# A three-layer cross network with gathers on one core: start-up, gathers and tower pieces rearranged, and ScalarE's copies turned round

## The reference

```python
def layer_stack(x0, W0, W1, W2):          # x0: (1024, 32, 16)
    xk, outs = x0, []
    for W in (W0, W1, W2):                # W: (32, 32 or 64, 64)
        xk = relu(einsum('bmd,bhd,mhk->bkd', x0, xk, W))
        outs.append(xk.sum(axis=2))
    return concatenate(outs, axis=1)      # (1024, 192)

e = stack([tbl_f[ids[:, f]] for f in range(32)], axis=1)
h = concatenate([layer_stack(e, W0, W1, W2), dense_ctx], axis=1)
y = relu(relu(h @ W_top1 + b_top1) @ W_top2 + b_top2) @ W_top3
```

## Time and profile before

| | |
|---|---|
| median of 3 runs | 656.71 us (653.54 to 657.66) |
| profiled execution, its own time | 655.87 us |
| its span in the trace | 654.1 us |
| busy: TensorE, VectorE, GpSimd, ScalarE | 574.3, 561.2, 474.0, 230.4 us |

### The profile page before, as it was taken

How to read it: one execution, slowest core, us unless ns; L and a number is a source line. 1 busy time by engine, 2 the same in 40 slices (tenths; PEclk the granted TensorE clock), 3 DMA queues, 4 the chain that set the end, 5 groups by cost and what they waited for, 6 DMA issues and landing times.

```text
span 654.1 us, 7255 instructions
## 1 busy us (share of the span) xinstructions
PE 574.3 (88%) x2752; PEld 202.9 (31%) x2752; DVE 561.2 (86%) x291; ACT 230.4 (35%) x425; POOL 474.0 (72%) x356
## 2 busy tenths in 40 slices
PE   0049778979999899989999899999999899989997
PEld 0013222213433234323433233323433233323434
DVE  0049787959999999989999899999999999999992
ACT  0130604315334334335324334335324334334401
POOL 6747388876888588876888588877888588724450
PEclk9998899989999999999999999999999999999999
DMA  5397919495396927795496927794496918693000
GB/s 161 106 402 264 368 33 383 175 365 189 118 383 228 404 59 265 273 364 190 137 394 220 387 54 282 259 374 178 160 398 225 356 52 312 249 388 136 0 2 0
DMA packets 54245, 151.96 MB, mean 232 GB/s; under 512 B 9697, under 2 KB 18913, under 8 KB 54210
## 3 DMA queue, kind: packets, MB, share of 16 engines
q1 hardware_dynamic: 46018, 149.39, 61.1%
q0 software_dynamic: 8192, 2.11, 2.8%
HBM read 147.26 MB, written 4.20 MB: 232 GB/s over the span
## 4 chain that ended last, share of the span: by engine, by line
PE 46%; DVE 18%; DMA 12%; issue 11%; POOL 11%; SPq 1%; ACT 0%; DVEq 0%; POOLq 0%
PE acc L507 40%; DVE zd L383 17%; DMA rolled<-x_scratch 10%; POOL emb L305 8%; POOL zg L317 3%; PE mlp L551 2%; DVE zpart L363 1%; PE mlp L542 1%; PE mlp L543 1%; SPq L269 1%; DMA emb<-tables_in,index 1%; PE mlp L558 1%; DMA x_scratch<-emb 1%; PE mlp L525 0%; DMA ids_sb<-ids_in 0%
## 5 line engine op out<-in xcount | busy, mean ns | idle before, releaser
L383 DVE TENSOR_TENSOR zd<-rolled,xk_ps 128x2048 f32<-128x2048 f32 x240 | 535.3, 2279 | 76.7 <-DMA rolled<-x_scratch 44.4
L507 PE MATMUL acc<-zd,w_sb 128*64 128x512 f32 x1664 | 390.5, 601 | 17.4 <-DVE zd L383 11.1
L305 POOL DMA_INDIRECT emb<-tables_in,index x256 | 245.3, 958 | 74.3 <-issue 62.8
L317 POOL TENSOR_TENSOR zg<-rolled,xk_sb 128x1024 f32<-128x1024 f32 x96 | 228.5, 2382 | 83.7 <-ACT xk_sb L416 71.1
L507 PEld LDWEIGHTS acc<-zd,w_sb 128*64 128x64 f32 x1664 | 116.2, 138 | 261.1 <-issue 197.6
L416 ACT ACTIVATE xk_ps<-acc 64x512 f32<-64x512 f32 x128 | 73.0, 570 | 182.7 <-PE acc L507 180.4
L507 PE MATMUL acc<-zg,w_sb 128*64 128x512 f32 x384 | 100.6, 599 | 7.3 <-POOL zg L317 7.3
L507 PE MATMUL acc<-zd,w 128*64 128x512 f32 x256 | 65.1, 631 | 46.9 <-DVE zd L383 46.9
L416 ACT ACTIVATE xk_sb<-acc 64x512 f32<-64x512 f32 x128 | 75.8, 592 | 3.1
L423 ACT ACTIVATE relu_ab<-acc 128x512 f32<-128x512 f32 x48 | 28.7, 599 | 51.3 <-PE acc L507 50.5
L507 PEld LDWEIGHTS acc<-zd,w 128*64 128x64 f32 x256 | 18.6, 144 | 88.3 <-issue 75.1
(11 more groups left out here) (46 smaller groups left out, 72.8 us busy)
## 6 DMA issues: line engine op xcount, KB each, us to landing
rolled<-x_scratch SPq DMA_DIRECT2D x256, 512.0 KB, 10.1
base<-x_scratch SPq DMA_DIRECT2D x16, 512.0 KB, 3.7
emb<-tables_in,index POOLq DMA_INDIRECT x256
x_scratch<-emb SPq DMA_DIRECT2D x32, 128.0 KB, 1.8
w_sb<-w_in SPq DMA_DIRECT2D x2, 512.0 KB, 4.5
wt<-wtop_in SPq DMA_DIRECT2D x1, 512.0 KB, 6.3
wt1a<-wtop_in SPq DMA_DIRECT2D x1, 256.0 KB, 5.1
w<-w0a_in SPq DMA_DIRECT2D x1, 160.0 KB, 2.3
```

Source lines behind the costliest of these rows:

```text
L305: pool.indirect_dma_start(emb[:, i % 2, c * DIM:(c + 1) * DIM], None, tables, bass.IndirectOffsetOnAxis(index[:, g:g + 1].bitcast(U32), 0) ...
L317: nc.gpsimd.tensor_tensor(zg[:, n % ZG_BUFS, :], rolled[:, s, j, :], xk_sb[:, s, :], ALU.mult).then_inc(zg_ready, 1)
L383: nc.vector.tensor_tensor(zd[:, n % ZD_BUFS, 0:w, :], rolled[:, s, j:j + w, :], repeated(xk_ps[:, s, :], w), ALU.mult).then_inc(zd_ready, 1)
L507: end = nc.tensor.matmul(acc[h * MAPS:(h + 1) * MAPS, s, :], weights, z[:, h * HALF:(h + 1) * HALF], start=(j + c == 0), stop=(i == len(me ...
```

## The change

The program does the same arithmetic but for two maps of (1,1,0), which move from GpSimd to VectorE: that phase is 14 + 2 maps instead of 12 + 4. In the start-up the gathers are distributed anew: behind the products of (0,1,0) four and six instead of three and five, behind the two of (1,1,0) three and four (before: three behind each of four), behind that of (0,2,1) four instead of three: 56 gathers by the end of the start-up instead of 58. `GATHERS_MORE` adds three gathers at the end of (a,1,1) in tiles 1 to 5. `evacuate` fills `xk_sb` ahead of `xk_ps`, except for layer 0 of an even stream (`s` there is the slot, 0 or 1). In the start-up ScalarE does squares(1) ahead of evacuate(0,1). In a tile it now does h1_to_sb ahead of evacuate(a,1) instead of behind it, and evacuate(b,1) last, behind h2_to_sb and y_to_sb. On TensorE the pieces of the tower come earlier: zsum behind entry 0 and mlp1 behind entry 4 of (a,1,1), mlp2 behind entry 2 and mlp3 behind entry 6 of (b,1,0). The sums of the last tile stay behind entry 6 of (15,2,0).

```diff
--- before.py
+++ after.py
@@ -46,7 +46,7 @@
 CHUNKS = {(0, 0): [(4, 0)], (0, 1): [(4, 0), (10, 2)], (0, 2): [(12, 4)],
           (1, 0): [(4, 0)], (1, 1): [(14, 2)], (1, 2): [(4, 1), (8, 3)]}
 
-CHUNKS_AT = {(0, 1): [(14, 2)], (0, 2): [(6, 1), (8, 1)], (1, 1): [(12, 4)], (STREAMS - 1, 2): [(12, 4)]}
+CHUNKS_AT = {(0, 1): [(14, 2)], (0, 2): [(6, 1), (8, 1)], (STREAMS - 1, 2): [(12, 4)]}
 
 ORDER = [(0, 0, 0), (0, 1, 0), (1, 0, 0), (0, 2, 0), (1, 1, 0), (0, 2, 1)]
 for _t in range(1, TILES):
@@ -60,8 +60,10 @@
 GATHERS_FIRST = 24
 GATHERS_EARLY = 8
 GATHERS_AFTER = {(0, 1, 1): [3, 3], (1, 1, 0): [3, 3], (0, 2, 0): [3, 3, 2, 2], (1, 2, 0): [3], (1, 2, 1): [2, 2, 3]}
-GATHERS_AFTER_AT = {(0, 1, 0): [3, 5], (0, 2, 0): [3], (1, 1, 0): [3, 3, 3, 3], (0, 2, 1): [3],
+GATHERS_AFTER_AT = {(0, 1, 0): [4, 6], (0, 2, 0): [3], (1, 1, 0): [3, 4], (0, 2, 1): [4],
                     (STREAMS - 1, 2, 0): [0, 0, 0, 0]}
+
+GATHERS_MORE = {(2 * t, 1, 1): 3 for t in range(1, 6)}
 
 
 def chunks(stream, layer):
@@ -338,6 +340,7 @@
                 for x, (_, n, j, _) in enumerate(PLAN.pool[q]):
                     product(q, n, j)
                     gathers(GATHERS_AFTER_AT.get(ORDER[q], GATHERS_AFTER.get((stream % 2, layer, part)))[x])
+                gathers(GATHERS_MORE.get(ORDER[q], 0))
 
         @block.vector
         def _(dve):
@@ -410,7 +413,11 @@
                 who, n, _, _ = PLAN.merged[end_of(stream, layer)][-1]
                 act.wait_ge(zd_used if who == "dve" else zg_used, n + 1)
                 if layer < 2:
-                    for dst, ready in ((xk_ps, xk_ps_ready), (xk_sb, xk_sb_ready)):
+                    copies = [(xk_ps, xk_ps_ready), (xk_sb, xk_sb_ready)]
+                    if (s, layer) != (0, 0):
+
+                        copies.reverse()
+                    for dst, ready in copies:
                         for h in range(2):
                             for copy in range(2):
                                 nc.scalar.activation(
@@ -447,8 +454,8 @@
             squares(0)
             evacuate(0, 0)
             base_to_ps(1)
+            squares(1)
             evacuate(0, 1)
-            squares(1)
             evacuate(1, 0)
             evacuate(1, 1)
             act.wait_ge(const_in, const_count)
@@ -463,11 +470,11 @@
                 squares(b)
                 evacuate(b, 0)
                 zsum_to_sb(m)
+                h1_to_sb(m)
                 evacuate(a, 1)
-                h1_to_sb(m)
-                evacuate(b, 1)
                 h2_to_sb(m)
                 y_to_sb(m)
+                evacuate(b, 1)
             evacuate(STREAMS - 2, 2)
             evacuate(STREAMS - 1, 2)
             act.wait_ge(last_z01_done, 1)
@@ -489,7 +496,7 @@
 
         @block.tensor
         def _(pe):
-            def phase(q, **between):
+            def phase(q, between={}):
 
                 stream, layer, part = ORDER[q]
                 s = stream % 2
@@ -515,10 +522,8 @@
                         for h in range(2):
                             nc.tensor.matmul(acc[h * MAPS:(h + 1) * MAPS, s, :], w0[:, L0CH, :],
                                              xk_sb[:, s, h * HALF:(h + 1) * HALF], start=False, stop=False)
-                    if "early" in between and i == 0:
-                        between["early"]()
-                    if "late" in between and i == len(merged) * 2 // 3:
-                        between["late"]()
+                    if i in between:
+                        between[i]()
 
             def half_sums(m, dst, layer):
                 for h in range(2):
@@ -573,10 +578,10 @@
                 q = 6 + 8 * m
                 for x in range(5):
                     phase(q + x)
-                phase(q + 5, late=lambda: zsum(m))
-                phase(q + 6, late=lambda: mlp1(m))
-                phase(q + 7, early=lambda: mlp2(m), late=lambda: mlp3(m))
-            phase(len(ORDER) - 1, late=last_sums)
+                phase(q + 5, {0: lambda: zsum(m), 4: lambda: mlp1(m)})
+                phase(q + 6, {2: lambda: mlp2(m), 6: lambda: mlp3(m)})
+                phase(q + 7)
+            phase(len(ORDER) - 1, {6: last_sums})
 
             m = TILES - 1
             pe.wait_ge(last_z01_sb, 1)
```

## The result

The changed kernel takes 634.19 us (median of 4 runs, 632.79 to 636.44) against 657.18 for the kernel before on the same chip (median of 4, 653.54 to 658.02): ratio 0.9664, interval 0.9617 to 0.9710. Timed again beside other runs it was 635.06 us, ratio 0.9674 (0.9644 to 0.9704). The forecast was 628.6 with a range of 623 to 636: the direction and the range held, my own narrower range of 624 to 633 didn't, and the gain was 23 us instead of 27.6 to 28. The profiled execution took 632.79 us, its span is 631.0.

A forecast was written before the change was run, and what follows sets the result against it. No engine was full, but VectorE and TensorE nearly were, so VectorE's small waits counted. Start-up 8.4, tiles 17.2 and end 2.0 made 27.6 us saved, giving 628.6 us; range 623 to 636, own range 624 to 633.

The forecast's parts named there:

- rival 1: Tiles 1 to 5: GpSimd's 71.2 us of work becomes the bound, 1.0 us more each, 634 us; chance 0.11.
- four signs of being right: (1,1) copies near 96; (3,0,0) second item near 134, load-bound; 70.2 us tiles without load waits; GpSimd never idle, tiles 1-5.
- Start-up: Before the second item of (3,0,0): earlier copies of (1,1) bring it from 142.72 to 134.3, gaining 8.4 us (6 to 11).
- Rival 4: Start-up gains nothing: TensorE's slow stretch lasts, copies of (1,1) stay at 104; 637 us; chance 0.03.
- ring-order rule: Loads of (3,0,0): one queue's descriptors are consumed in order per DMA engine; if it held, the item starts at 130.5, not 134.3.
- Steady tiles: Six repeating two-stream tiles: each falls to 70.2 us, saving 2.9 us, 17.2 us in all.
- The store and loads follow until the squares of the even stream stop them: Odd streams in a tile: earlier gathers bring store and loads forward to 267.7, 7 us sooner, so VectorE's 1.4-1.7 us wait goes.
- The tower: Tile's tower pieces on TensorE: starting them earlier cuts VectorE's zd-buffer waits from 1.5 us to 0.6, one stall of 0.55.
- Rival 2: Steady tiles: two or three zd-buffer stalls stay, tiles of 71.8 us, 639.6 us in all; chance 0.07.
- GpSimd's load: Tiles 1 to 5: GpSimd's work grows from 67.4 to 71.2 us, slipping about 1.1 us a tile, at no cost.
- 3: Rival: gathers wait for stores queued behind loads that need GpSimd's products; slower than before, up to 689 us; chance 0.02.
- The end: After the last steady tile: the merged tower pieces of (15,2,0) end at 62.4 instead of 64.4, saving 2.0 us (0.5 to 2.5).

The follow-up runs named there:

- the first experiment: The kernel before with only the start-up edits (14+2 maps in (1,1,0), its gathers, squares(1) first): 680.24 us, ratio 1.0343.
- the first two experiments: The kernel before with the start-up edits alone, 680.24 us (ratio 1.0343); the changed kernel without the three extra gathers per tile, 674.15 us (1.0240).

## Why the prediction was right, and where it was off

The range held partly by luck. Its upper part was there for rival 1, which didn't happen; what took the time instead was a cost that the prediction had put at nothing (below). Of its four signs of being right two came true, the copies of (1,1) near 96 and the item near 134. Load waits stayed, and GpSimd stood idle in tile 1.

- **Start-up: forecast 8.4 us, measured 9.2.** The replay held step by step: squares at 60.49 (60.2), the item of (0,2,0) at 70.35 (70.75), copies of (1,1) at 95.64 (96.0), the product at 98.16 (98.5), the gather at 116.32 (116.65), the load-bound item at 133.51 (134.3). One step was wrong and cost nothing: TensorE didn't restart at its lower clock after its idle time ahead of 72.79 (below). Nor did the turned copies carry it; the first experiment has the gain without them. Rival 4 is out.
- The estimate that the prediction set beside the ring-order rule of the Trainium skill ("DMA: Bandwidth & Descriptors", section "Queues, rings and completion order"), 130.5 for that item, came out 3.0 us early. But "the trace disagrees" was said of the wrong thing. The rule is that descriptors of one queue are consumed in ring order on each DMA engine, and the trace agrees: of stream 3's loads the second lands at 128.90, the third to fifth at 130.73, 132.01 and 133.38, in the order of their issue, and the item starts at 133.51. What failed is the estimate of five loads' bytes at 320 GB/s from the first issue. The base load of the same size, issued at 121.02, moves ahead of them and lands at 124.81; from the first issue at 121.96 to the fifth landing it is 11.4 us and not 8.2.
- **Steady tiles: forecast 17.2 us, measured 12.1. This is the term that failed**, and in it the step "The store and loads follow until the squares of the even stream stop them", with its conclusion that the wait of 1.4 to 1.7 us goes. I followed the semaphores and took the landing of a gather and a store to be as quick as in the rows before, 2.4 and 2.2 us. Those rows were measured when the DMA engines had emptied. Moved forward (by 4 us in tile 1, 10 in tile 2, 24 and more from tile 4 on), the last gather and the store fall among the even stream's 16 loads or behind them (8.4 MB at 380 GB/s in the window from 170, so 22 us by estimate). The gather took 5.5 to 5.9 us in tiles 1 to 3; the store still took 2.2 in tile 1, but 6.5 in tile 2 and 12 to 13 in tiles 3 to 6. They win 0.7 to 3.3 us of T (60.6 to 58.0 against 61.3) where VectorE needed 2.8. Halving those loads gave back the whole term: tiles of 70.2.
- *The tower:* one stall of 0.49 us, forecast 0.55. Rival 2 is out. But its gain isn't additive: put back late it cost 1.3 us a tile against the 70.2, and took the load waits away.
- *GpSimd's load:* no wait of TensorE for a zg beyond 0.3 us in the tiles. Rival 1 is out, and 3 too: no gather waited for a store. The slip cost nothing, as said. In tile 1 GpSimd had slack that I hadn't counted on: it waited 5.86 us ahead of 141.50 for a rolled load, and 0.9 us for xk_sb in tiles 1 and 2.
- **What I didn't see at all** is how near the kernel before stood to a cliff. I read its 73 us as VectorE's work plus small waits; the first two experiments show a tile paced by the position of one gather. The change removes two gathers of lead and adds three a tile: without the second it would be 2.4% slower than the kernel before. My rivals had no such case; GATHERS_MORE was, in my text, one of four edits, and is worth 39 us.
- **The end:** 1.8 us, forecast 2.0.
- The sum of errors: +0.8 in the start-up, -5.1 in the tiles, -0.2 at the end; 27.6 becomes 23.1.

## What to carry to other kernels

When a transfer is moved earlier, look up what the DMA engines do at its new time, slice by slice: the mean share of a period (0.7 here) says nothing, and a landing time read from a row holds only for the load it was read under. When no engine is full and a period is longer than any engine's work, look for a ring through several engines and price an edit by what it does to the ring's weakest position, not by its own length. Waits of a fraction of a us trade places: remove the second before you judge the first.

## What the runs showed of the hardware

- A stream's last gather landed (from its start to the issue of the store that waits for it) in 2.4 us at a DMA share of 0.06, and in 5.5 us at a share of 1.03 (401 GB/s), both in tile 2. The store of 2 x 128 KB took 2.2 us at a share of 0.40 and 6.5 us at 0.85.
- Right behind 16 loads of 512 KB in the same queue, such a store took 12 to 14 us; right behind 16 of 256 KB, 5 to 7 us. Issued on another engine's queue 1.8 to 2.6 us later, it took 7.8 to 9.0 us behind the full loads.
- Loads of one queue landed in the order of their issue, about 1.3 to 1.4 us apart while the engines were full (512 KB each: 130.73, 132.01, 133.38).
- TensorE stood still for 2.45 us and went on at its higher clock (2.4 GHz: eight matrix multiplications in 1.94 us), where it had come back at the lower one (1.2 GHz, four in 1.98 us) after 3.23 us. The length of the stop alone doesn't tell: in the same run it stood still for 3.31 us ahead of 131.45 and went on at a granted clock of 1.00 until 132.5; only then came the lower one (0.62 from 132.5 to 133.5). The row of the first case:

```profile
72.79 1.94 PE L514 MATMUL acc<-zd,w_sb 128*64 128x512 f32 x8 [2.45 <-DVE zd L386]
```
